# Splitting six PSUM banks four to two between the two score products of an attention

## What is computed

```
# layer 0, cross-attention: 16 heads of 16, 1024 keys
qh, kh, vh = heads(q @ wq.T + bq), heads(ctx @ wk.T + bk), heads(ctx @ wv.T + bv)
scores = einsum('bhqd,bhkd->bhqk', qh, kh) / 4
attn = softmax(where(mask == 0, -1e9, scores), axis=-1)
out = einsum('bhqk,bhkd->bhqd', attn, vh) @ wo.T + bo
# layer 1, hard cross-attention: 16 query heads, one key head, 512 keys
qp = q @ Wq.T
idx = argmax(einsum('bld,bmd->blm', qp, ctx), axis=-1)
mk, mv = split(take(ctx, idx) @ Wkv.T, 2)
attn = softmax(einsum('bhld,bmd->bhlm', heads(qp), mk) / 4)
out = einsum('bhlm,bmd->bhld', attn, mv) @ Wc.T
```

## Time and profile before

| | us |
|---|---|
| median of 3 runs | 1014.28 (1014.04 to 1014.97) |
| the profiled execution | 1017.49 |
| its span, first to last instruction | 1015.7 |
| TensorE busy | 910.3 (90%) |
| VectorE busy | 640.8 (63%) |
| ScalarE busy | 469.6 (46%) |
| GpSimd busy | 321.6 (32%) |
| cross-attention, from its first score product to its last value product | 158.8 to 388 |
| hard cross-attention, likewise | 749 to 878 |

### The profile page before, as it was taken

The page is one execution under the profiler, slowest core; times in us unless marked ns, Lnnn a source line. Parts: engine busy times, 40 slices in busy tenths (PEclk is TensorE's granted clock), DMA queues, the critical chain, the costliest instruction groups (busy, mean ns, idle before and its releaser), DMA issues. The chain is left out here.

```text
span 1015.7 us, 12766 instructions
## 1 busy us (share of the span) xinstructions
PE 910.3 (90%) x4067; PEld 457.8 (45%) x4071; DVE 640.8 (63%) x1323; ACT 469.6 (46%) x928; POOL 321.6 (32%) x328
## 2 busy tenths in 40 slices
PE   5879987999999987499899999999988999859996
PEld 2435553433332334366655555555432332434565
DVE  4756666888889933445436555655579998444754
ACT  3776544577777772022134333332215777333321
POOL 7225635400000001156426555545230000115933
PEclk9989998999999998599989999999999999958999
DMA  5030016022212901723393000000100000066200
GB/s 152 1 141 14 1 46 106 14 50 49 49 45 53 329 4 48 292 94 113 108 363 122 1 1 1 0 1 1 54 27 1 33 33 1 1 227 210 78 17 26
DMA packets 41653, 73.77 MB, mean 73 GB/s; under 512 B 8964, under 2 KB 27780, under 8 KB 40436
## 3 DMA queue, kind: packets, MB, share of 16 engines
q1 hardware_dynamic: 36372, 59.68, 18.8%
q0 software_dynamic: 4400, 13.11, 4.0%
q10 hardware_dynamic: 816, 0.17, 0.1%
HBM read 49.67 MB, written 10.49 MB: 59 GB/s over the span
## 5 line engine op out<-in xcount | busy, mean ns | idle before, releaser
L1076 DVE TENSOR_REDUCE c_amx<-PS 128x1 f32<-128x512 f32 x256 | 158.8, 684 | 30.4 <-PE PS L976 30.2
L1169 ACT ACTIVATE c_aE<-PS 128x512 f32<-128x512 f32 x256 | 132.5, 603 | 47.1 <-PE PS L988 46.9
L1827 POOL TENSOR_SCALAR s_Pn<-s_Pr,s_rs 128x512 f32<-128x512 f32 x64 | 99.9, 1564 | 102.2 <-DVE s_rs L1855 102.0
L71 POOL TENSOR_SCALAR rstd<-mv 128x4 f32<-128x4 f32 x8 | 1.9, 232 | 335.1 <-DVE mv L94 335.0
L976 PE MATMUL PS<-c_aKs,c_aQs 99*128 99x512 bf16 x256 | 96.2, 388 | 6.8 <-DMA c_aQs<-area 4.0
L1914 ACT ACTIVATE s_Pr<-PS,s_nmx 128x512 f32<-128x512 f32 x64 | 44.0, 687 | 116.3 <-DVE s_nmx L1848 116.3
L988 PE MATMUL PS<-c_aQs,c_aKs 99*128 99x512 bf16 x256 | 94.5, 380 | 3.5 <-ACT c_aE L1169 2.3
L1846 DVE TENSOR_REDUCE s_mx<-PS 128x1 f32<-128x512 f32 x64 | 44.2, 691 | 69.3 <-PE PS L1961 69.3
L1076 DVE TENSOR_REDUCE h_amx<-PS 128x1 f32<-128x512 f32 x128 | 79.4, 683 | 8.5 <-PE PS L976 8.2
L1169 ACT ACTIVATE h_aE<-PS 128x512 f32<-128x512 f32 x128 | 67.7, 601 | 21.5 <-PE PS L988 21.2
L999 PE MATMUL PS<-c_aE,c_VB 128*17 128x512 f32 x512 | 67.4, 598 | 0.1
(11 more groups left out here) (440 smaller groups left out, 1687.7 us busy)
## 6 DMA issues: line engine op xcount, KB each, us to landing
area<-in_e_w SPq DMA_DIRECT2D x16, 512.0 KB, 9.3
area<-in_g_w SPq DMA_DIRECT2D x8, 1024.0 KB, 15.6
c_aKs<-area SPq DMA_DIRECT2D x48, 128.0 KB
g_B<-in_g_b SPq DMA_DIRECT2D x1, 4096.0 KB, 13.7
c_aQs<-area SPq DMA_DIRECT2D x48, 64.0 KB
h_aQs<-h_QP SPq DMA_DIRECT2D x48, 64.0 KB
early<-in_ctxT SPq DMA_DIRECT2D x2, 1024.0 KB, 7.7
e_B<-in_e_b SPq DMA_DIRECT2D x1, 2048.0 KB, 11.3
```

Of the source, the lines that this page charges most:

```text
L1076: dve.tensor_reduce(self.mx[:, qt, j, half:half + 1], PS[:, n % MB, :], AX.X, ALU.max).then_inc(self.max_done, 1)
L1169: act.activation(self.E[kt % 2][:, j, :], PS[:, MB + x % XB, :], ACT.Exp, scale=0.25).then_inc(self.exp_done, 1)
L1827: pool.tensor_scalar(Pn[g % NPB][:, :], Pr[g % NPB][:, :], rs[:, g % NPB:g % NPB + 1], None, ALU.mult).then_inc(pn_ready, 1)
```

## The change

Four banks (0 to 3) for the score products and two (4, 5) for the transposed products. The ring of the key, query and value products loses bank 3, which now belongs to the score products, and the spare products of hard cross-attention go to bank 4. Nothing else changes: the same instructions stand in the same order on every engine, with other bank numbers and other counts to wait for.

```
-MB, XB = 3, 3
+MB, XB = 4, 2

@@ class EarlyKeys
     NK = 1024
-    RING = (6, 5, 3, 4, 7)
+    RING = (6, 5, 4, 7)
     FIRST = 2

@@ def hard_cross_stage
                 if c == TB - 1 and j == 2:
-                    spare_matmuls(pe, sh, 3, 10)
+                    spare_matmuls(pe, sh, 4, 10)
```

## The result

| | before | after |
|---|---|---|
| median | 1014.16 us (1014.03 to 1014.97, 4 runs) | 1029.62 us (1027.24 to 1037.53, 4 runs) |
| ratio | | 1.0161, 95% interval 1.0126 to 1.0195 |
| the profiled execution | 1017.49 us | 1028.51 us |
| its span | 1015.7 us | 1026.7 us |
| mean granted clock of it | 0.953 | 0.962 |

The change makes the kernel 1.6% slower; the forecast was 1029.8 us. The two profiled executions lie only 11.0 us apart, the medians 15.5 us: the profiled execution of before was one of its longer ones.

What follows compares the result with a forecast made beforehand. TensorE alone was taken to set the pace. Cross-attention +12.7 us (steps +15.8, prologue -3.1) and hard cross-attention +2.8 us sum to +15.5 us on 1014.28: 1029.8 us, range 1024 to 1036 us.

Steps and rivals of the forecast that it cites:

- A full step: Step with score products: third and fourth transposed products wait for exponentials, +0.27 us, period 2.82 to 3.09 us.
- The last unit: Steps without score products, transposed products back to back: waits for exponentials add 0.49 us to 2.38 us.
- The boundary pair of cross-attention: Two steps at a unit boundary: +0.11 us to 6.48 us, copies of the tails hiding part of the stalls.
- The hard boundary pair: Two steps at a hard cross-attention unit boundary: fourth score bank removes a wait, 7.00 to 6.49 us, gain 0.51.
- The prologue of cross-attention: Score groups before the steps: fourth score bank shortens each from 3.11 to 2.59 us, gain 3.1 us in all.
- Rival C: Clock stays up ahead of the cross-attention prologue, saving about 3 us: 1026.8 us; chance 12%.
- The ring's wait: Projections before the scores: sixth key chunk waits for the third's copy, hidden by idle time, otherwise 1.5 us.
- Hard cross-attention: Whole hard attention: +2.8 us, from prologue -0.2, first boundary +0.1, boundaries -2.6, full steps +3.5, last steps +2.0.
- Rival B: Clock falls in the attentions because stalls break TensorE's stream: +75 us, 1105 us; chance 3%.
- A: Rival, faster: waits for maxima are what costs, fewer transposed-product banks are free: 1004.9 us; chance 4%.
- D: Rival: exponentials after a stall don't overlap, 0.38 us a step in place of 0.27: +8 us, 1038 us; chance 7%.
- The sign "idle for exponentials up by over 20 us": Expected in the profile after: products' idle time for exponentials rises by over 20 us.

Runs made afterwards that it cites:

- e_three_two: Kernel before with three score banks, only two transposed-product banks, and its ring of five kept: 1036.45 us, ratio 1.0210.
- e_ring_only: Kernel before with only the ring of key banks shortened from five to four: 1013.74 us, ratio 0.9993.
- e_fill_idle: Kernel before, ring of five, plus ten unread spare products in the idle time ahead of the first score product: 1014.45 us, ratio 1.0004.
- e_cross_only: Kernel before with four and two banks and the ring of four in cross-attention alone: 1025.13 us, ratio 1.0094.
- e_prologue_four: Kernel before with four score banks in the two prologues alone, three and three after them, ring of four: 1014.01 us, ratio 0.9985.
- e_two_four: Kernel before with the opposite split, two score banks and four transposed-product banks: 1053.00 us, ratio 1.0377.
- e_hard_only: Kernel before with four and two banks in hard cross-attention alone, ring of five in cross-attention: 1017.15 us, ratio 1.0017.
- e_order: Changed kernel with two transposed products first, then score products before the third, in all steps but a unit's first: 1020.18 us, ratio 1.0034.
- e_wide_last: As e_order, plus transposed products rotating over four banks in each attention's last unit: 1009.00 us, ratio 0.9953 against the kernel before.

## Why the prediction was right

- **What bounds the kernel.** TensorE, with T's distance to its bank's last exponential as the next limit: right. e_three_two shows it by itself.
- **A full step, 3.09 us, T2 at 1.07 and T3 at 1.555:** 3.09, 1.07 and 1.56. The second steps of a unit went from 3.31 to 3.58 us, by the same 0.27. The fourth steps of six units rose by 0.2 only (4.72 to 4.91, and 2.89 to 3.09 where no value products of 1.99 us are in them): before, their S3 had already waited 0.08 us for VectorE, which had just normalised. The prediction counted them as full steps.
- **The last unit, +0.49 us a step (2.87):** 2.86, and 4.69 where it was 4.20. The first step without S rose by 0.09 (3.16 to 3.25), 0.10 forecast.
- **The boundary pair of cross-attention, +0.11 us (6.48):** 6.57 where it was 6.37, so +0.20. T1 waits for the tails' copies until 4.08 us after the first S (4.07 forecast), but T2 then follows 0.71 us after T1, not 0.62. Over six boundaries 0.6 us.
- **Steps of cross-attention in all, +15.8 us:** +15.9. That it fits to 0.1 us is in part luck: 0.5 us too little for the boundaries and 0.1 for the first two steps stand against 0.5 too much for the fourth steps and 0.2 for the last unit.
- **The hard boundary pair, -0.51 us (6.49):** 6.57, -0.43. But the reason was only half right. I gave this gain to the fourth S bank. e_three_two has half of it without that bank: its boundary step is 3.52 us where before had 3.79. VectorE comes to maximum 0 of that step 4.1 us after the start of the step before in both kernels (794.29 in before, 808.58 in e_three_two), and T's stalls make the step before 0.27 us longer, so TensorE waits that much less for VectorE. The bank itself is worth 0.2.
- **The prologue of cross-attention, -3.1 us (bounds -1.5 and -3.8):** -3.8 from the bank (28.9 to 25.1). The mis-sized term is the number of groups: I took seven, and one at half clock at 0.2 us. At full clock all nine gain 0.52 us, 4.7 in all, three key copies (not two) take back 0.9, and the sum comes to the upper bound.
- **Rival C, the clock ahead of the prologue, 12% and 3 us.** It came, on top of the forecast, and is worth 2.3 us of the stretch, shown by e_ring_only and e_fill_idle (2.1 us in the first group, 0.2 in the second). The first T comes 6.1 us earlier after the first S, where 3 us were forecast. I had both pieces in the text, the idle time of 3.98 us and the ring that moves TensorE's last work 1.5 us on, and gave the combination too small a chance.
- **The ring's wait, 1.5 us, hidden:** 1.44 us and hidden.
- **Hard cross-attention, +2.8 us:** -0.9 and +4.4 in the profiles, +3.5. The prologue gained 0.9 us (0.2 forecast), and most of it is given back in the first steps, by the longer wait for VectorE's keys (1.94 us for 1.34): the first two value groups stand 5.32 us apart, not 4.44 (in e_three_two 4.39). From the first S to the end of that wait it is 28.1 us for 28.3, so the 0.2 us of the forecast, set by VectorE. I had not looked at who is late there. The other steps then sum to the forecast but for the boundary pairs: -2.1 us for five instead of -2.6. The steps of before and of the other kernels with (3, 3) and the old order scatter from 107.2 to 107.8 us, all of it in the first two steps. In e_cross_only, e_ring_only and e_prologue_four (107.6 to 107.8) TensorE runs these at half clock for 5 to 6 us; in before it doesn't, and in e_fill_idle for 3 us only (both 107.2).
- **Rival B.** In cross-attention the granted clock is 1.00 from 189 to 400 us, with two breaks of the stream in each step. In hard cross-attention it is 0.57 from 770 to 774 us, in the prologue, and 1.00 from there to the end (774 to 889). The kernel before has the same fall in its prologue (0.57 from 762 to 766), where no T runs yet, so the change doesn't bring it. The Trainium skill, "TensorE: Matmul & The Clock Gate", section "A second HAM failure mode: psum-queue depth-cycling", speaks of a clock that toggles under short breaks from cycling through PSUM banks. T's stalls show no such thing here, nor do the breaks of up to 0.3 us of e_two_four (1.00 from 189 to 410 and from 802 to 910 us). **A** fell with e_three_two. **D** fell too: T3 stands 0.49 us after T2, so the exponentials overlap behind a stall as elsewhere.
- **The sign "idle for exponentials up by over 20 us"** came (+72 us), but it was a poor sign: most of it is weight loads, and for products alone (3.2 us more) the stalls vanish in the drawn lengths. The distances between starts were the right one.

The forecast of +15.5 us met a measured +15.5 us of the medians, yet the stretches say only +13.3: 2.3 us less for the clock of rival C, 0.7 less for the banks of the prologue, 0.7 more for hard cross-attention. That the medians are nearer to the forecast than the stretches is within their interval, and no proof of it; that the number was met to 0.2 us is luck, while the 0.27 and 0.49 us a step, which carry it, were met and shown.

**What stays open.** For after, e_three_two, e_two_four, e_cross_only, e_hard_only, e_ring_only, e_order and e_wide_last the sum of the stretches lies within the interval. For e_prologue_four it lies 1.8 us below the interval, for e_fill_idle 0.8 us. In both the gain is nearly all in the cross prologue, and 2.3 us of it are the clock. One reading is that the clock at that point doesn't always fall in executions that were not profiled, so that there is less to gain; another is that the clock falls elsewhere in exchange. Each kernel but after has one profiled execution, and the timed ones have no trace, so neither is shown.

## What to carry to other kernels

The banks that a queue of products needs follow from one comparison: the time from a product's start until its bank is free again (0.42 us to the start of the exponential, 0.60 for it, 0.05 to the next product) against the time in which TensorE comes round to that bank; here a bank less cost just the difference, in every full step, whatever the shares of busy time say. Before giving banks away, change the order so that the reader's time is filled with other products, and let the split differ by stage: banks that one queue leaves idle in the last unit are free for the other (1009.0 us against 1015 and 1030). Read such stalls from the distances between starts, since the profile draws a product longer than the distance to the next.

## What the runs showed of the hardware

An idle time of 3.98 us ahead of the first S was followed by a granted clock of 0.57 from 159 to 166 us. All four kernels with the ring of five and nothing in that idle time (3.06 to 4.02 us) show such a fall: 0.57 to 0.70 from 155 to 163 us. In the seven profiled executions with the ring of four, where it is split into 1.44 us and 1.43 to 2.06 us with 3.7 us of products between, the clock stayed at 1.00, and ten products of 2.32 us in it did the same. ScalarE's exponentials stand 0.488 us apart though each lasts 0.597, behind a stall as well as in a full queue; VectorE's maxima 0.60 us apart with 0.680 each.
